# Attention steps of a two-layer transformer kernel on Trainium2: the projection into the other PSUM bank, the norm's transpositions behind the scores, and the second half of the weighted values ahead of a row tile's transpositions

## What is computed

```python
x = x + tanh(g_xattn[0]) * L0_xattn_ref(_layernorm(x), ctx_1024, ...)
x = x + tanh(g_ffn[0])   * L0_ffn_ref(_layernorm(x), ...)      # 8 experts by position
x = x + tanh(g_xattn[1]) * L1_xattn_ref(_layernorm(x), ctx_1024, ctx_1024, ...)
x = x + tanh(g_ffn[1])   * L1_ffn_ref(_layernorm(x), ...)      # 7 routed experts and a shared one

# attention: 16 heads of 16, 77 context rows as keys and values
scores = einsum('bhqd,bhkd->bhqk', q, k) / sqrt(16)
out = einsum('bhqk,bhkd->bhqd', softmax(scores), v) @ W_o.T + b_o
```

## Time and profile before

| | |
|---|---|
| runs | 869.77 us median of 3 (866.08 to 872.19) |
| profiled execution | 871.15 us, of it 869.4 us span |
| PE busy | 827.6 us, 95% of the span |
| DVE, ACT, POOL busy | 62%, 51%, 32% |
| attention of layer 0, of layer 1 | up to about 146 us; about 244 to 388 us |
| PE waits for L1111 (copy of transpositions) | 7.5 us in 7 places |
| PE waits at L619 for L1503 (x_new) | 3.4 us in 7 places |

### The profile page before, as it was taken

The page is one execution under the profiler, slowest core; times in us unless marked ns, Lnnn a source line. Parts: engine busy times, 40 slices in busy tenths (PEclk is TensorE's granted clock), DMA queues, the critical chain, the costliest instruction groups (busy, mean ns, idle before and its releaser), DMA issues.

```text
span 869.4 us, 16981 instructions
## 1 busy us (share of the span) xinstructions
PE 827.6 (95%) x5604; PEld 725.1 (83%) x5604; DVE 536.9 (62%) x1171; ACT 444.2 (51%) x1033; POOL 276.3 (32%) x329
## 2 busy tenths in 40 slices
PE   8799989999978999879999999999999999999997
PEld 6567757999956777668888999989999999989986
DVE  4578854556585888366446574636557473645658
ACT  3567756777665777432323452616345361625331
POOL 5234424887763452145561002020100102020130
PEclk9999999999998999989999999999999999999999
DMA  6333273876520000301113422314233231413252
GB/s 206 90 93 129 71 283 120 254 234 216 169 66 9 7 6 6 99 0 37 56 51 93 131 72 78 115 41 121 72 97 92 64 107 54 132 38 101 63 192 100
DMA packets 72647, 86.17 MB, mean 99 GB/s; under 512 B 29226, under 2 KB 45292, under 8 KB 72470
## 3 DMA queue, kind: packets, MB, share of 16 engines
q1 hardware_dynamic: 65382, 69.55, 27.0%
q10 hardware_dynamic: 3664, 9.46, 2.9%
q0 software_dynamic: 3552, 6.55, 2.3%
HBM read 63.28 MB, written 23.58 MB: 100 GB/s over the span
## 4 chain that ended last, share of the span: by engine, by line
PE 79%; DVE 8%; ACT 4%; issue 3%; SPq 2%; ACTq 1%; DMA 1%; POOL 0%; DVEq 0%; POOLq 0%
PE score L298 13%; PE score L299 13%; PE score L300 13%; PE bank_p L304 11%; PE bank_p L305 6%; PE bank L641 2%; PE bank_p L610 2%; DVE mx L1484 2%; PE bank L623 2%; PE bank L619 2%; PE score L599 1%; PE bank L633 1%; SPq L388 1%; PE bank L620 1%; PE bank L626 1%
## 5 line engine op out<-in xcount | busy, mean ns | idle before, releaser
L1272 ACT ACTIVATE silu<-score 128x366 f32<-128x366 f32 (+1 forms) x144 | 72.5, 504 | 265.5 <-PE score L300 265.5
L304 PE MATMUL bank_p<-w_both,hid_hi 128*122 128x512 f32 (+1 forms) x432 | 152.6, 396 | 0.5 <-DVE hid_lo L1675 0.5
L1667 DVE TENSOR_TENSOR prod<-silu,score 128x366 f32<-128x366 f32 (+1 forms) x144 | 81.9, 569 | 113.3 <-ACT silu L1272 112.9
L298 PE MATMUL score<-xe_hi,w_both 128*128 128x366 f32 x448 | 147.5, 329 | 0.0
L299 PE MATMUL score<-xe_lo,w_both 128*128 128x366 f32 x448 | 147.4, 329 | 0.0
L300 PE MATMUL score<-xe_hi,w_both 128*128 128x366 f32 x448 | 147.2, 329 | 0.0
L2187 POOL DMA_INDIRECT slots_out<-yh,home_of x42 | 40.8, 972 | 331.4 <-DVE yh L1824 329.3
L305 PE MATMUL bank_p<-w_both,hid_lo 128*122 128x256 f32 (+1 forms) x432 | 121.0, 280 | 0.0
L304 PEld LDWEIGHTS bank_p<-w_both,hid_hi 128*122 128x122 f32 (+1 forms) x432 | 79.5, 184 | 21.4 <-DVE hid_lo L1675 1.6
L2003 POOL TENSOR_TENSOR w_both<-raw,w_both 128x512 fp32r<-128x512 f32 x62 | 82.6, 1360 | 34.0 <-ACT w_both L1054 27.2
L298 PE MATMUL score<-act_hi,w_both 128*128 (+2 forms) x256 | 87.9, 343 | 3.7 <-DVE prod L1667 3.7
(11 more groups left out here) (250 smaller groups left out, 1659.2 us busy)
## 6 DMA issues: line engine op xcount, KB each, us to landing
raw<-w_second_d SPq DMA_DIRECT2D x108, 256.0 KB, 2.7
raw<-w_first_d SPq DMA_DIRECT2D x56, 256.0 KB, 3.4
yh<-slot_rows SPq DMA_DIRECT2D x7, 674.6 KB
slot_rows<-yh ACTq DMA_DIRECT2D x5, 771.0 KB, 3.4
slots_out<-yh ACTq DMA_DIRECT2D x5, 512.0 KB, 4.3
slot_rows<-yh SPq DMA_DIRECT2D x3, 771.0 KB, 5.8
v_rest<-values SPq DMA_DIRECT2D x128, 1.6 KB
raw<-w_first_d ACTq DMA_DIRECT2D x8, 256.0 KB, 3.3
```

Of the source, the lines that this page charges most:

```text
L298: nc.tensor.matmul(o, a_hi, b_hi, start=start, stop=False)
L304: nc.tensor.matmul(o, a_hi, b.rearrange("p c d -> p (c d)"), start=start, stop=False)
L1272: nc.scalar.activation(silu[0:rows_n, buf, 0:width], src, ACT.Silu).then_inc(silu_done, 1)
L1667: nc.vector.tensor_tensor(prod[0:rows_n, buf, 0:width], silu[0:rows_n, buf, 0:width], up, ALU.mult).then_inc(gu_free, 1)
```

## The change

The change reorders each attention step on three engines and moves one output to another PSUM bank. No instruction is added or taken away.

- TensorE: the projection of g - 2 goes to bank 0 (it was bank 1). Unit 3 of g - 1 is transposed ahead of it, not behind; the wait for the copy to `stage` stands ahead of it. The first half of the values no longer waits for `x_new`. The first norm's transpositions stand behind scores 2 and 3, behind a wait for `x_new`. The second half of the values stands ahead of unit 1's transpositions, which are now the last piece of a step.
- ScalarE: the copies follow: unit 3 ahead of `exps` 0, the copy to `xn_t` behind the reciprocal of `dt` 0, unit 1 behind `exps` 3.
- VectorE: `norm_stats` of g + 2 moves from ahead of `add_attention` to behind the maxima of unit 2, ahead of `normalise_out` of `dt` 0.
- The end of layer 1: the last projection and the second norm's transpositions of g = 14 stand ahead of the third shared gate/up.

```diff
--- before.py
+++ after.py
@@ -672,16 +672,16 @@
                     prob_transposes(g - 1, 2)
                 if three:
                     norm2_t(g - 3)
-                if two:
-                    project_out(g - 2, bank[1])
                 if some:
                     prob_transposes(g - 1, 3)
+                if three:
+                    pe.wait_ge(stage_ready, staged(layer, g - 3))
+                if two:
+                    project_out(g - 2, bank[0])
                 if start:
                     pe.wait_ge(wv_in, 16)
                     values(0, 0, bank[1])
-                if three:
-                    pe.wait_ge(stage_ready, staged(layer, g - 3))
-                if not final_step:
+                if n == 0:
                     norm_t(g + 1)
                 if start:
                     pe.wait_ge(v_ready, 1)
@@ -694,8 +694,6 @@
                     pe.wait_ge(wa_in, 16)
                     pe.wait_ge(v_ready, 3)
                     pe.wait_ge(ones_done, 2)
-                if two:
-                    pe.wait_ge(x_new, g - 1)
                 if some:
                     weighted_values(g - 1, 1 - par, 0, batches)
                 if layer == 1 and three:
@@ -707,16 +705,20 @@
                 if layer == 1 and n == 0:
                     pe.wait_ge(y0_done, 1)
                     pe.wait_ge(y0_late, 2)
+                if two and not final_step:
+                    pe.wait_ge(x_new, g - 1)
+                if some and not final_step:
+                    norm_t(g + 1)
                 prob_transposes(g, 0)
                 if some and not final_step:
                     queries(g + 1)
+                if some:
+                    pe.wait_ge(ot_ready, KT * g - 1)
+                    weighted_values(g - 1, 1 - par, 1, batches)
                 prob_transposes(g, 1)
                 if start:
                     pe.wait_ge(v_ready, 2)
                     values(0, 2, bank[1])
-                if some:
-                    pe.wait_ge(ot_ready, KT * g - 1)
-                    weighted_values(g - 1, 1 - par, 1, batches)
 
             def warm_array():
 
@@ -789,10 +791,10 @@
                     shared_gate_up(0, 1)
                     pe.wait_ge(ot_ready, KT * g + 1)
                     weighted_values(g, 1, 1, placed(1, B - 1))
-                    shared_gate_up(0, 2)
                     project_out(g, bank[1])
                     pe.wait_ge(logit_done, B - 2)
                     norm2_t(g - 1)
+                    shared_gate_up(0, 2)
                     route_logits(g - 1, bank[0])
                     shared_gate_up(0, 3)
                     pe.wait_ge(logit_done, B - 1)
@@ -1138,8 +1140,8 @@
                 if three:
                     norm2_t(g - 3, layer == 0 and n == 3)
                 if some:
+                    probs_t(g - 1, 3)
                     exps(g, 0)
-                    probs_t(g - 1, 3)
                 if three:
                     high(layer, g - 3, b - 3)
                 if layer == 0 and final_step:
@@ -1170,9 +1174,9 @@
                     nc.scalar.activation(flat(w_hi[:, bass.ds(b + (FT - 3), 1)]), flat(raw_by[:, bass.ds(b - 3, 1)]), ACT.Copy).then_inc(hi2, 1)
                 if some and not final_step:
                     queries(layer, g + 1)
-                probs_t(g, 1)
                 exps(g, 2)
                 exps(g, 3)
+                probs_t(g, 1)
                 if layer == 0 and n == 0:
                     values(0, 2, bank[1])
                 if layer == 0 and n in (0, 1):
@@ -1536,21 +1540,18 @@
                     normalise_out(g - 2, 1)
                 if not (layer == 1 and n == 0):
                     max_sub(g, 0, start)
+                    max_sub(g, 1, start)
                 if start:
-                    max_sub(g, 1, start)
                     scale_rows()
-                if ahead:
-                    norm_stats(layer, b + 2, False)
                 if two:
-                    add_attention(layer, b - 2, g - 2, bank[1])
-                if not start and not (layer == 1 and n == 0):
-                    max_sub(g, 1, start)
-                if two:
+                    add_attention(layer, b - 2, g - 2, bank[0])
                     norm2_stats(b - 2, g - 2, layer == 0 and n == 2)
                 if layer == 1 and three:
                     dve.wait_ge(s_psum, 4 * g + 4)
                     keep_logits(b - 3, step_logits)
                 max_sub(g, 2, start)
+                if ahead:
+                    norm_stats(layer, b + 2, False)
                 if some:
                     normalise_out(g - 1, 0)
                 max_sub(g, 3, start)
```

## The result

The changed kernel takes 882.54 us in the median of 4 runs (881.25 to 884.04), the kernel before beside it 870.31 (4 runs, 866.08 to 872.19). The ratio is 1.0156, its 95% interval 1.0123 to 1.0189 (the quotient of the two medians, 1.0141, lies inside it). The profiled executions differ by 11.3 us of span (880.7 against 869.4).

A forecast was written before the change was run, and what follows sets the result against it. TensorE, nearly full in steady steps, was taken as the bound, waiting only for late pieces. Terms 4.2 + 2.6 + 1.8 + 2.4 + 0.1 + 0.6 + 0.5 = +12.2 us on 871.15, less 1.4, gave 882 us, range 873 to 889.

The forecast's parts named there:

- layer 1's steady steps: Layer 1, steps 3 to 6: same +2.1 us as layer 0's order, routing adding 1.04 a step to both orders.
- the end: End of layer 1: projection fills 1.8 us of idle time but the third gate/up starts later; +0.5 us (-0.2 to +1.6).
- the stretch between the layers: Last step of layer 0 is set by another block of ScalarE loads before and after: +0.1 us.
- The step's layout: Steady layer 0 step clocked from unit 1's transposes: halves of 6.78 and 6.73, 13.51 us against 13.05; 2.1 a layer.
- T3: Unit 3's transposes, with only four transposes between them and unit 2's: 0.45 us lost in each step's first half.
- sign of being wrong: Wrong if layer 1's steady steps take under 14.1 us, or layer 0's steps grow no more than layer 1's.
- zero_slots: Layer 0, steps 3 to 6: its DMA issues on ScalarE delay the reciprocal and unit 2's copy, 0.65 us each; +2.6 us.
- Steps 1 and 2 of layer 0: ScalarE's loads delay the reciprocal and unit 3's transposes, and the projection runs at the lower clock: +2.4 us (0 to +4).
- Layer 1, steps 1 and 2; last step: Steps 1 and 2: 20.24 us against 18.43, +1.8. Last step: unit 2's transposes follow unit 1's directly, +0.6 (0 to 1.4).
- A: Rival: nothing takes the place of the removed wait, steps are their pieces alone, 12.14 us; -6 us, 864; chance 12%.
- B: Rival: only the round trips cost, zero_slots' issues and step 1's loads hide as before; +6.6 us, 876; chance 22%.
- C: Rival: the new gaps bring the clock to its lower level in steady steps; +12 us more, 894; chance 6%.

The follow-up runs named there:

- e_t3: Changed kernel with unit 3's transposes back behind the projection on TensorE: ratio 1.0248 to the kernel before, 890.1 us.
- e_zero: Changed kernel with ScalarE issuing the two zero_slots DMAs ahead of the copy of unit 1's transposes in layer 0: ratio 1.0128 to the kernel before, 880.3 us.
- e_loads: Changed kernel with ScalarE's four loads at the end of layer 0's step 1 issued at the end of step 0: ratio 1.0157 to the kernel before, 881.5 us.
- e_stats: Changed kernel with norm_stats back ahead of add_attention on VectorE: ratio 1.0127 to the kernel before, 880.0 us.
- e_t1: Changed kernel with unit 1's transposes back ahead of the values' second half, their copy ahead of the last two exponential pairs: ratio 1.0061 to the kernel before, 873.9 us.
- e_tail: Changed kernel with the third shared gate/up back ahead of the last projection and second norm's transposes: ratio 1.0186 to the kernel before, 885.1 us.
- e_t1_stats: Changed kernel with both unit 1's transposes back ahead of the values' second half and norm_stats back ahead of add_attention: ratio 1.0002 to the kernel before, 869.1 us.
- b1: Kernel before with only the projection's other bank, pieces placed so that each round trip is covered: ratio 1.0007 to the kernel before, 869.3 us.

## Why the prediction was right, point by point

The forecast of 882 us holds, and the mechanism with it: the round trips, the issues and the late statistics cost more than the wait gave back. That the sum came within 0.9 us is partly luck: layer 1's steady steps were 1.6 us too low, and the end and the stretch between the layers 1.1 and 0.7 us too high.

**The step's layout.** Right. With the 0.65 us of issue that I charged, my clock from T1 had T3 at 3.63, the projection at 4.18, values 0 at 6.02 and the second pair at 7.98; step 5 has 3.69, 4.29, 6.08 and 8.04 from T1 at 86.81 (0.70 us ahead of the pair at 87.51). The second half was to be 6.73 and is 6.89: values 1 was forecast 4.12 and is 4.16 behind the pair, but T1 and the scores behind it took 0.69 instead of 0.55. What was wrong in it is the reason for one term: T3 cost nothing by itself, since the projection waited for `stage` just as long (e_t3). Neither sign of being wrong appeared: layer 1's steady steps took 14.9 us, not under 14.1, and layer 0's four grew by 4.9 us, layer 1's by 3.7.

**zero_slots.** Right: 2.6 forecast, 2.5 shown by e_zero. On the path the issues cost 0.62 us a step, and without them (e_zero) three of the four steps took 13.51, 13.52 and 13.18 us, where the layout had 13.51, 13.51 and 13.17. The Trainium skill (DMA: Bandwidth & Descriptors, section Issuing engines are not separate DMA queues) calls the time of an issue usually small relative to the transfer; read as nothing to pay, it would have made the term 0, and the measurement decides against that reading.

**Steps 1 and 2 of layer 0.** The mechanism was right: the loads ahead of the reciprocal, T3's wait, and the lower clock behind it. The size (2.7 for 2.4) was right by luck, as two of its parts were off and cancelled. In the changed kernel:

```profile
43.03 0.41 ACTq L359 DMA_DIRECT2D wa<-attn_w_d  x1
...
43.62 0.38 ACT L1119 ACTIVATE o_t<-bank 128x256 f32<-128x256 f32 x1 [1.78 <-issue]
...
45.25 1.30 PE L610 MATMUL bank_p<-ident,prob 128*128 128x128 f32 x5 [2.53 <-ACT prob_t L1113]
...
46.35 3.62 PE L633 MATMUL bank<-wa,o_t 128*128 128x256 f32 x8
```

T3 waited 2.53 us, and the projection behind took 3.62 us where it takes 1.99 at the upper clock. One guess was off: L359 took only 0.41 us where it had taken 2.02, so that L1119 started 9.1 us behind the pair, the low end of 9.1 to 10.5. Why is not shown. The other was the clock, for which I had charged 1.2 to 1.6 us, the projection alone. From T3 to the second pair of step 2 (windows of the changed kernel, then of e_loads):

```profile
45.25:52.47 7.22, 7.22 (x33) 5.22 (x34) 4.56 (x11) 2.32 (x6) 0.00 (x0) 0.58 0.32 92
47.72:51.98 4.26, 4.26 (x34) 3.09 (x34) 4.12 (x10) 2.28 (x6) 0.00 (x0) 1.00 0.21 48
```

The same pieces, all without a wait, took 7.22 us at a clock of 0.58 and 4.26 at 1.00: the clock cost 3.0 us.

**Layer 1, steady steps.** The mis-sized term: 3.7 instead of 2.1. The step that failed is "so 2.1 there too". VectorE has two more operations for the second norm there (L1466 and L1480, L1462 and L1476 before; 47.3 us busy of 55.7 then), and I looked for the effect of the moved `norm_stats` only at values 1. It delays the second norm as well, and with it `stage` and the projection; from the second pair of a step the first of the two starts 0.9 us later than before (306.44 less 300.77; before, 298.52 less 293.79):

```profile
309.55 0.66 PE L560 MATMUL bank<-ident,xn 128*128 128x128 f32 x4 [0.17 <-DVE xn L1480]
...
311.10 1.99 PE L633 MATMUL bank<-wa,o_t 128*128 128x256 f32 x8 [0.31 <-ACT stage L1089]
...
320.25 0.67 PE L619 MATMUL bank<-prob_t,v_rest 128*128 128x256 f32 x2 [0.30 <-DVE o_t L1501]
```

0.17, 0.31 and 0.30 us in a step. A second thing makes the norm late: the same operations last longer, though they are not changed. In the changed kernel, then before:

```profile
306.44 1.89 DVE L1466 SCALAR_TENSOR_TENSOR xn<-residual,mv,row 128x256 f32<-128x256 f32 x2
306.55 1.50 POOL L2001 TENSOR_TENSOR w_both<-raw,w_both  x1
...
298.52 0.93 DVE L1462 SCALAR_TENSOR_TENSOR xn<-residual,mv,row 128x256 f32<-128x256 f32 x2
```

L1466 takes 1.89 us instead of 0.93, and L1480 1.13 instead of 0.88: 1.2 us a step. GpSimd now works through nearly all of both (L2001 and L1988, 306.55 to 309.21), since it gets the statistics later; before, it was done at 298.77. In e_stats, where GpSimd's two products also lie over it, L1466 takes 1.42. That the overlap is what lengthens them fits these traces and is not shown by a run of its own.

e_stats took 2.8 us off these four steps, e_t1 nothing: in layer 1 VectorE's lateness covers the round trip of T1 completely, so the two are no sum.

**Layer 1, steps 1 and 2; last step.** 1.4 for 1.8 and 0.4 for 0.6: near, and each from two single executions.

**The end.** Forecast +0.5, measured -0.6 between two single executions. The waits were seen as described, only larger:

```profile
381.93 1.99 PE L633 MATMUL bank<-wa,o_t 128*128 128x256 f32 x8 [1.41 <-DVE o_t L1501]
...
388.27 0.63 PE L560 MATMUL bank<-ident,xn 128*128 128x128 f32 x4 [4.35 <-DVE xn L1480]
```

Before, the third gate/up waited for 3.67 us; now the projection waits for 1.41 and the second norm for 4.35. e_tail did not settle what the move is worth.

**The rivals.** A (nothing replaces the wait) is refuted by the waits' summary and by e_t1_stats: even with T1 and the statistics back, the copy to `stage` behind T2 and the pair of norm and queries take back the 0.6 us that the wait had cost. The Trainium skill (Perfetto Trace Analysis, section Optimizing Tensor Performance) wants independent matmul groups to rotate through PSUM banks, so that the copy of one lies over the next; in b1, where a group for another bank stands between any two for one bank, the undisturbed steps 3 and 5 of layer 0 took 12.55 and 12.71 us against 12.97 and 13.12, so the trace agrees, as far as TensorE's own steps go. B is refuted by e_zero. C did not come: the clock stood at 1.00 in all steady windows, with waits of 1.05 us in them.

## What to carry to other kernels

Before moving a piece to remove a wait, write down for each pair of writes to one PSUM bank how far apart they stand and which piece covers the copy between them; a wait of 0.5 us is soon paid back by a pair that loses its cover. Ask which instructions stand behind the moved one on its own engine, DMA issues above all: here the same two were free behind one piece and cost 0.62 us a step behind another. Look also at what the moved one feeds on a third engine, and what that will then run beside. And before making the busiest engine faster, look at the queue that feeds it: here some 0.4 us a step was won on TensorE in b1, and waits for the value loads took it back.

## What was not expected of the hardware

A queue's issuing can be a bound with little data in flight: SyncE spent 13.3 us on the twelve small loads of a batch in layer 0 (b1, 58.54 to 71.88) at a DMA share of 0.33, with hardly a pause between batches, and one of TensorE's waits (1.29 us in step 7) went when six of these issues were taken off it. An issue's length varies: L359 in step 1 of layer 0 lasted 2.02 us before and 0.41 in the changed kernel, L356 0.40 and, once, 1.73 (e_stats); off the path this does not matter, on it it does. Four loads issued 13 us earlier on ScalarE put the arrival of the first values 4.1 us later (e_loads), 3.2 of it behind the last issue of those values' own loads. And a wait of 2.53 us cost more behind it than in itself: T3, the projection and values 0's first pieces ran at the lower clock and took 3.0 us more, and the whole stretch was 4.8 us longer than in e_loads, where T3 waited 1.8 us less.
